# Layer 1 attention: context projections moved beside the layer norm, low parts taken by TensorE, four PSUM slots ahead of the first scores

## The reference

```python
x = x + jnp.tanh(g_xattn[1]) * _L1_xattn_ref(_layernorm(x), ctx_1024, ln_g, ln_b, Wq, Wkv, Wm, Wo, bo)

def _L1_xattn_ref(x, memories, ln_g, ln_b, Wq, Wkv, Wm, Wo, bo):
    xn = (x - mu) * rsqrt(var + EPS) * ln_g + ln_b      # a second norm, over the first
    q, kv, mem = xn @ Wq, xn @ Wkv, memories @ Wm       # mem: 6404 rows, from the context alone
    k = concatenate([k, mem]); v = concatenate([v, mem])
    attn = softmax(q @ k.T * 64 ** -0.5)                # 1024 x 7428 for each head
    return (attn @ v) reshaped @ Wo + bo
```

## Time and profile before

| | us |
|---|---|
| median of 3 runs | 5230.36 (5229.31 to 5230.93) |
| the profiled execution, its own time | 5229.35 |
| its span in the profile | 5227.6 |
| PE busy | 4813.3 (92%) |
| DVE busy | 4069.5 (78%) |
| ACT busy | 3357.1 (64%) |
| POOL busy | 1961.0 (38%) |

### The profile page before, as it was taken

The page is one execution under the profiler, slowest core; times in us unless marked ns, Lnnn a source line. Parts: engine busy times, 40 slices in busy tenths (PEclk is TensorE's granted clock), DMA queues, the critical chain, the costliest instruction groups (busy, mean ns, idle before and its releaser), DMA issues. The chain is left out here.

```text
span 5227.6 us, 76770 instructions
## 1 busy us (share of the span) xinstructions
PE 4813.3 (92%) x26366; PEld 1882.8 (36%) x26366; DVE 4069.5 (78%) x4870; ACT 3357.1 (64%) x6623; POOL 1961.0 (38%) x1522
## 2 busy tenths in 40 slices
PE   8938999999999999999994699999998699999997
PEld 5623454545445454544442222222222222222222
DVE  7646767677676767677776699999995599999996
ACT  3314565666666566656651388888885288888886
POOL 0015878787787878788782100000000100000000
PEclk9978999999999999999996799999998699999998
DMA  1024334242333334242210311111110211111110
GB/s 36 5 88 120 95 95 112 63 123 54 110 75 99 95 90 117 55 126 56 52 30 16 81 32 29 29 29 29 29 23 2 79 29 29 29 32 32 29 23 6
DMA packets 171390, 298.23 MB, mean 57 GB/s; under 512 B 39060, under 2 KB 108576, under 8 KB 167392
## 3 DMA queue, kind: packets, MB, share of 16 engines
q1 hardware_dynamic: 169420, 292.95, 22.0%
q10 hardware_dynamic: 1584, 0.37, 0.0%
HBM read 187.39 MB, written 101.25 MB: 55 GB/s over the span
## 5 line engine op out<-in xcount | busy, mean ns | idle before, releaser
L1856 ACT ACTIVATE a_prob<-ps 128x512 f32<-128x512 f32 (+1 forms) x3264 | 1699.4, 602 | 289.0 <-PE ps L1736 284.2
L1914 DVE TENSOR_REDUCE a_mx<-ps 128x1 f32<-128x1024 f32 x1536 | 1815.1, 1220 | 70.6 <-PE ps L1748 55.0
L1283 POOL TENSOR_TENSOR tot_p<-tot_p,prob 128x512 f32<-128x512 f32 (+1 forms) x922 | 1300.6, 1411 | 353.6 <-ACT prob L1141 267.6
L1748 PE MATMUL ps<-a_K,a_Q 59*128 59x512 bf16 (+1 forms) x3328 | 1094.7, 386 | 56.6 <-DMA a_Q<-q_stack_dram 44.7
L1141 ACT ACTIVATE prob<-ps 128x512 f32<-128x512 f32 (+1 forms) x1512 | 801.4, 609 | 511.7 <-PE ps L1007 510.7
L1736 PE MATMUL ps<-a_Q,a_K 59*128 59x512 bf16 (+1 forms) x3264 | 988.7, 383 | 55.3 <-ACT a_prob L1856 49.1
L1772 PE MATMUL ps<-a_prob,a_V 128*9 128x512 f32 x6528 | 872.1, 596 | 10.9 <-ACT a_acc L1840 10.9
L1006 PE MATMUL ps<-QA,KA 128*128 128x512 f32 (+1 forms) x1888 | 841.7, 446 | 0.0
L1018 PE MATMUL ps<-prob,V 128*64 128x512 f32 x3024 | 801.1, 599 | 0.7 <-ACT prob L1141 0.7
L1007 PE MATMUL ps<-QB,KB 128*128 128x512 f32 (+1 forms) x1888 | 746.6, 395 | 0.0
L1224 DVE TENSOR_TENSOR tot_d<-tot_d,prob 128x512 f32<-128x512 f32 x539 | 619.4, 1149 | 146.0 <-ACT prob L1141 129.5
(11 more groups left out here) (419 smaller groups left out, 4341.4 us busy)
## 6 DMA issues: line engine op xcount, KB each, us to landing
a_K<-k_stack_dram SPq DMA_DIRECT2D x128, 300.2 KB
k_hi_dram<-hi_s SPq DMA_DIRECT2D x112, 256.0 KB, 2.1
k_lo_dram<-lo_s SPq DMA_DIRECT2D x112, 256.0 KB, 2.4
KA<-k_hi_dram SPq DMA_DIRECT2D x64, 384.0 KB, 4.3
KA<-k_lo_dram SPq DMA_DIRECT2D x64, 384.0 KB, 5.6
KB<-k_hi_dram SPq DMA_DIRECT2D x64, 384.0 KB, 6.6
k_bf_dram<-bf_s SPq DMA_DIRECT2D x112, 128.0 KB, 1.8
KM<-k_bf_dram SPq DMA_DIRECT2D x32, 448.0 KB, 5.5
```

Of the source, the lines that this page charges most:

```text
L1283: nc.gpsimd.tensor_tensor(tot_p[0:r, u % 2, :], tot_p[0:r, u % 2, :], p, ALU.add).then_inc(totalled_p, 1)
L1748: last = nc.tensor.matmul(c.banks(slot(step) + half)[:, 0:k], Q[u % 3][MROW:MROW + ROWS, j * P:(j + 1) * P], K[(u // HALVES) % 2][MROW:MRO ...
L1856: nc.scalar.activation(prob[0:r, batch % 2, t % BATCH, :], c.banks(n % 3)[0:r, :], ACT.Exp, scale=SCALE).then_inc(exped, 1)
L1914: nc.vector.tensor_reduce(mx[:, u % 2, j, i % FULL:i % FULL + 1], c.banks(slot(step), 2), AX.X, ALU.max).then_inc(maxed, 1)
```

## The change

- The jobs of the context come first (k = 0 to 12), then q and k of x (13 to 16). `norm` is no longer a phase of its own for layer 1: DVE norms in the phase of the projections, while PE, ACT and POOL run the context's jobs.
- Since DVE is taken, the low part of the 13 context jobs of the first pair comes from PE: `take_hi` multiplies hi_s with the negative identity (`neg`, kept in QA[1]) and adds it to the job's PSUM; ACT copies what is left (`round_lo`). The 4 jobs of x still go by DVE.
- The two square roots stand in ACT's order behind jobs 3 and 7 (STD_BEHIND). Behind job 12 PE transposes h (`turn_h`), then waits for DVE's copy to hT.
- Up to the last maximum step of unit 0 there are four slots: banks 4 and 5, 6 and 7, 0 and 1, 2 and 3; after it again two.
- SP waits for KM and QM of head 0 to land before it issues `load_q` and the segments.
- gain and shift lie in fin_s.

```diff
+    MEM_JOBS = len(jobs)
+    jobs += [(W_Q, c.hT, a, n, [(a, 0, n)]) for a, n in chunks_of(N)]
+    jobs += [(W_K, c.hT, a, n, [(MEM + a, 0, n)]) for a, n in chunks_of(N)]
+    STD_BEHIND = (3, 7)
...
     def slot(n):
-        return 4 + 2 * (n % 2)
+        return (4, 6, 0, 2)[n % 4] if n < WIDE_SLOTS else 4 + 2 * (n % 2)
+
+    def before_slot(n):
+        return n - 4 if n < WIDE_SLOTS else n - 2
...
-            norm(c, gain, shift)
...
                 load_max(0)
+                sp.wait_ge(max_in_0, 96)
                 load_q(0)
...
+                def take_hi(k):
+                    m = jobs[k][3]
+                    pe.wait_ge(hi_out, k + 1)
+                    nc.tensor.matmul(c.banks(slot(slot_no["k", k]))[:, 0:m], neg, hi_s[k % DEPTH][:, 0:m],
+                                     start=False, stop=True, skip_group_check=True).then_inc(rest_ready, 1)
+
+                def turn_h():
+                    bank = take_slot(slot_no["turn", 0])
+                    pe.wait_ge(h_ready, 1)
+                    for t in range(QT):
+                        last = nc.tensor.transpose(c.banks(bank, 2)[:, t * P:(t + 1) * P], c.h[:, t, :], c.ident[:])
+                    last.then_inc(slotted, 1)
+                    pe.wait_ge(hT_ready, 1)
+
                 for k in range(JOBS):
+                    if k == MEM_JOBS:
+                        turn_h()
                     project(k)
-                    if k < GROUPS:
-                        project_v(0, k)
+                    if v_with(k) is not None:
+                        project_v(0, v_with(k))
+                    if k < MEM_JOBS:
+                        take_hi(k)
...
+                def round_lo(k):
+                    n, m = slot_no["k", k], jobs[k][3]
+                    act.wait_ge(rest_ready, k + 1)
+                    nc.scalar.copy(lo_s[k % DEPTH][:, 0:m], c.banks(slot(n))[:, 0:m]).then_inc(v_out, 1)
...
                 for k in range(JOBS):
                     round_hi(k)
-                    if k < GROUPS:
-                        take_v(0, k)
+                    if k < MEM_JOBS:
+                        round_lo(k)
+                    if v_with(k) is not None:
+                        take_v(0, v_with(k))
+                    if k in STD_BEHIND:
+                        root(STD_BEHIND.index(k))
...
-                for k in range(JOBS):
+                for k in range(MEM_JOBS, JOBS):
                     cut_lo(k)
```

More of the change, by code:

```diff
@@ L654, in l1_attention @@
     k_hi, k_lo, k_bf, q_hi, q_lo, q_bf = scratch
-    jobs = [(W_Q, c.hT, a, n, [(a, 0, n)]) for a, n in chunks_of(N)]
-    jobs += [(W_K, c.hT, a, n, [(MEM + a, 0, n)]) for a, n in chunks_of(N)]
+    jobs = []
     for a, n in chunks_of(S):
@@ L710, in takes_slot @@
         slot_no[kind, what] = len(slot_no)
-        by_act, count = kind in ("v", "fin"), [0, 0] if not freed else list(freed[-1])
+        by_act = kind in ("v", "fin") or (kind == "k" and what < MEM_JOBS)
+        count = [0, 0] if not freed else list(freed[-1])
         count[by_act] += 1
@@ L715, in l1_attention @@
     for k in range(JOBS):
+        if k == MEM_JOBS:
+            takes_slot("turn", 0)
         takes_slot("k", k)
-        if k < GROUPS:
-            takes_slot("v", (0, k))
+        if v_with(k) is not None:
+            takes_slot("v", (0, v_with(k)))
     for n in range(STEPS + LEAD):
         takes_slot("max", divmod(n, STEPS))
+    WIDE_SLOTS = slot_no["max", (0, STEPS - 1)] + 1
     for u in range(UNITS):
@@ L839, in l1_attention, with _ @@
-        fin_s, den = sb("fin_s", [P, CH]), sb("den1", [P, UQ])
+        fin_s, den = sb("fin_s", [P, CH]), sb("den1", [P, UQ])
+        gain, shift = fin_s[:, 0:D], fin_s[:, D:2 * D]
+        neg = QA[1][:, 0:P]
+        row_sum, var, rstd, tmp = (c.stat[:, i, :] for i in range(4))
+        with phase(nc, "loaded") as (block, loaded):
+            @block.sync
+            def _(sp):
+                sp.dma_start(gain, w["ln_g"].partition_broadcast(P)).then_inc(loaded, 16)
+                sp.dma_start(shift, w["ln_b"].partition_broadcast(P)).then_inc(loaded, 16)
+                sp.dma_start(bo[:], w["bo"].partition_broadcast(P)).then_inc(loaded, 16)
+                for base in (0, DH):
+                    sp.dma_start(Wo_twice[0][base:base + DH, :], w["Wo"][0:DH, :]).then_inc(loaded, 16)
+                sp.wait_ge(loaded, 16 * 9)
+            @block.scalar
+            def _(act):
+                act.dma_start(weights[0][:, W_Q, :], w["Wq"][:, 0:P]).then_inc(loaded, 16)
+                act.dma_start(weights[0][:, W_K, :], w["Wkv"][:, 0:P]).then_inc(loaded, 16)
+                act.dma_start(weights[0][:, W_V, :], w["Wkv"][:, HEADS * DH:HEADS * DH + P]).then_inc(loaded, 16)
+                act.dma_start(weights[0][:, W_M, :], w["Wm"][:, 0:P]).then_inc(loaded, 16)
+                nc.scalar.activation(neg, c.ident[:], ACT.Copy, scale=-1.0)
+            @block.vector
+            def _(dve):
+                nc.vector.memset(ones_col[:], 1.0)
+                nc.vector.memset(V[:, TILES - 1, :], 0.0)
+                for tile in QB:
+                    nc.vector.memset(f32(tile[DH:P, :]), 0.0)
+            @block.gpsimd
+            def _(pool):
+                nc.gpsimd.memset(f32(KB[DH:P, :]), 1.0)
@@ L873, in store @@
                         sp.dma_start(hi_to[p, :, to:to + m], f32(hi_s[k % DEPTH][:, frm:frm + m])).then_inc(done, 16)
-                    sp.wait_ge(released, freed[slot_no["k", k]][0])
+                    if k < MEM_JOBS:
+                        sp.wait_ge(v_out, freed[slot_no["k", k]][1])
+                    else:
+                        sp.wait_ge(released, freed[slot_no["k", k]][0])
                     for to, frm, m in parts:
@@ L946, in take_slot @@
                 def take_slot(n):
[L947 to L948 removed]
+                    if before_slot(n) >= 0:
+                        by_dve, by_act = freed[before_slot(n)]
                         if by_act:
@@ L1150, in take_extra, with root @@
                         take_fin(what)
+                def round_lo(k):
+                    n, m = slot_no["k", k], jobs[k][3]
+                    act.wait_ge(rest_ready, k + 1)
+                    nc.scalar.copy(lo_s[k % DEPTH][:, 0:m], c.banks(slot(n))[:, 0:m]).then_inc(v_out, 1)
+                def root(r):
+                    act.wait_ge(var_ready, r + 1)
+                    nc.scalar.activation(rstd, var, ACT.Sqrt).then_inc(std_ready, 1)
                 for k in range(JOBS):
                     round_hi(k)
-                    if k < GROUPS:
-                        take_v(0, k)
+                    if k < MEM_JOBS:
+                        round_lo(k)
+                    if v_with(k) is not None:
+                        take_v(0, v_with(k))
+                    if k in STD_BEHIND:
+                        root(STD_BEHIND.index(k))
                 for n in range(STEPS + LEAD):
```

42 lines of the change are left out of this document (39 added, 3 removed).

## The result

Four runs before gave a median of 5230.64 us (5229.31 to 5230.93), four of the changed kernel 5193.75 us (5192.08 to 5195.90). The forecast was 32.

A forecast was written before the change was run, and what follows sets the result against it. PE bounds the long loop of units, so an earlier first score moves the end equally. The terms brought that score from 438.41 to 405.7, 32.7 us, less 0.7 for DVE and POOL: 5198 us, range 5193 to 5206.

The forecast's parts named there:

- The ring through ACT: Context jobs: ACT's rounding, PE's product, ACT's low part and values follow each other and set a period of 2.4 us.
- Term 1: Start of the projections: PE starts at about 321.8 us, once POOL's memset releases the barrier behind `loaded`.
- Term 2: Thirteen context jobs: 2.4 us per job, second rounding at 327.4, rounding of job 12 at 353.8.
- Term 3: PE's transposes of h behind job 12: at full clock without waiting for h, jobs on x start at 357.1.
- The cover: Norm beside the context jobs: y is cleared by 350.5 and needed by 354.5, 4 us to spare.
- The rival that the clock falls at the turn: PE idles 1.6 us for DVE's copy; transposes and last jobs at half clock cost 1.0 + 5.9: 5205; chance 0.09.
- Term 4: Last four jobs and stores: about 5.9 us of jobs, last rounding at 363.0, KM issued at 367.0.
- Term 5: Loads of KM and QM: alone they need 7.3 us instead of 8.99; PE starts the maxima at 374.3.
- Term 6: First maxima: with four slots DVE is the bound, 27.0 us for 33.25, gain 6.2.
- The price on DVE: Norm beside POOL's casts: passes stretch by some 3 us, mostly in the cover; 0.7 us taken off the gain.
- The 3 us at the root: Second square root: if each DVE pass waited for a whole cast, ACT would wait up to 3 us: 5201.
- The list of rivals: Chances beside the forecast's 0.64: maxima unchanged 0.08, clock 0.09, norm bound 0.08, more gain 0.06, slower 0.03, no change 0.02.

The follow-up runs named there:

- e1: The kernel before with only the four slots, up to the last maximum step of unit 0: 5210.85 us against 5228.68.
- e2: The changed kernel with the two slots of before everywhere: 5212.27 us, ratio 0.9971 to the kernel before.
- e3: The changed kernel with the norm back in a phase of its own ahead of the projections: 5213.39 us, ratio 0.9973 to the kernel before.
- e11: The changed kernel with KM's context part loaded early in three pieces and POOL's memset of KB's lower half moved out of the first phase: 5192.44 us.
- e5: The changed kernel with the second square root behind job 10 instead of job 7: 5200.96 us, ratio 0.9944 to the kernel before.
- e7: The changed kernel with KM's context part loaded in two transfers ahead of job 14's stores: 5197.32 us, ratio 0.9937 to the kernel before.
- e4: The changed kernel without SP's wait for KM and QM before queries and segments are issued: 5196.45 us, ratio 0.994 to the kernel before.
- e6: The changed kernel with two slots in the projections and four from the first maximum step on: 5206.36 us, ratio 0.9957 to the kernel before.
- e9: The changed kernel run once more, unaltered, as a base for later runs: 5193.27 us against 5227.00 for the kernel before.

## Why the prediction was right, and where its sizes were off

- **The mechanism holds, but for the first term.** The ring through ACT set the jobs, the turn was covered, DVE bounded the maxima, and the loop of units gave nothing back. The two parts of the change are shown apart and add up: four slots alone 17.2 us (e1), all else alone 17.8 (e2), both 35.1. The path by e1 and e3 (17.2, then -3.4, then 21.3) gives 35.1 too, but it must, since each step starts where the last one ends.
- **Term 1, PE's start, was right by luck.** Forecast 7.0, measured 7.19. The prediction has the barrier released by POOL's memset; e11 shows that it is released by SP's wait for its transfers, which ends soon after.
- **Term 2, the thirteen jobs, was mis-sized.** I had 2.4 us per job; it is 2.15. The product takes 0.50 us and not the 0.41 of L1006, but ACT's low part, values and next rounding start 0.48 us apart and not 0.61. The eleven periods took 23.85 us with the two roots in them instead of 26.4, 2.6 less, and the second rounding was 0.6 earlier after PE's start than forecast. I had read ACT's durations where the distances of their starts were wanted; the earlier trace rows hold the lesson for PE, where the job's matmuls last 1.10 us and the values start 0.93 after them.
- **Term 3, the turn, was right, and in part by luck.** Transposes at full clock without a wait, 2.4 us from their start to PE's next job. h was ready at 350.4 us, 3.7 ahead. The cover was needed: in e5 a wait of 2.5 us came with 2.6 more through the clock. The rival that the clock falls at the turn, which had a chance of 0.09, came true in e7, whose kernel is the same up to there: of eight traces in which PE did not wait for h, seven kept the full clock behind the turn's 1.37 us and e7 did not. It cost 1.7 us there and not the 6.9 that the rival had, since the clock was back after two jobs.
- **Term 4, last jobs and stores.** The four jobs took 5.5 us (forecast 5.9), but from the last rounding to KM's issue there are 5.2 and not 4.0; the prediction's own parts (0.58, 0.72, two issues of 0.4, 2.3) add up to 4.4. The jobs follow each other in 1.75 us now, and the stores arrive at 86% of what the transfers can do, at 315 GB/s (second row of the stages above); in e5, where they come more slowly, the same step took 4.0.
- **Term 5, the load, failed.** I gave 7.3 us to the load alone; it takes 8.75, and 8.97 in company (e4). The 1.25 MB take 5.9 us at about 210 GB/s, where I had 5.6, and about 1.6 us pass before the first data, where I had 1.7; what I left out is the 1.2 us from the last data to PE's start. SP's wait does not pay.
- **Term 6, the maxima.** 25.6 us, forecast 27.0: DVE is the bound, and e1 and e6 give the same 25.6 with other work before it. The size was off for the reason of term 2. The same 46 instructions keep DVE busy for 24.83 us and not 26.17, with hardly another duration (0.69 us for the mean of L1197 in both, 1.22 for the reductions of two banks): one starts before the last has ended, now that none waits for PE.
- **The price on DVE was too high.** I had taken 0.7 us. POOL and DVE do meet: a pass of the norm that took 1.23 us alone takes 1.51 at two places where a cast falls on it, and the casts, 0.61 us in the median before, take up to 1.69:

```profile
347.66 1.23 DVE L1315 TENSOR_TENSOR h<-h,fin_s 128x1024 f32<-128x1024 f32 x1
...
347.68 1.69 POOL L1356 CAST bf_s<-hi_s 128x512 bf16<-128x512 f32 x1 [1.54 <-ACT hi_s L1125]
...
348.92 1.51 DVE L1316 TENSOR_TENSOR h<-h,fin_s 128x1024 f32<-128x1024 f32 x1
...
349.83 1.08 POOL L1356 CAST bf_s<-hi_s 128x512 bf16<-128x512 f32 x1 [0.47 <-ACT hi_s L1125]
```

The first cast starts with a DVE pass and ends 0.48 us after it, the next DVE pass ends 0.28 us late. This is the exclusive interface that the Trainium skill describes ("SBUF — State Buffer", section "Who interferes with whom": a DVE instruction with two SBUF inputs against a GpSimd one that reads SBUF); the trace agrees with it, with 1.69 for 0.61 us. But it is mostly POOL that waits, whose casts have room, and the root found its variance ready (344.64) when ACT came (344.76). The 3 us at the root that the rule could have cost did not come, though with only 0.12 us to spare.

The errors go both ways, and that half of them cancel is luck. Gains over the forecast: 3.1 us in the first jobs (term 2), 0.2 at the turn, 0.4 in the last four jobs, 1.4 in the maxima, 0.1 behind them, and the 0.7 of the price. Losses: 0.2 in PE's start, 1.2 in the stores, 1.4 in the load. The difference is the 3 us by which the shift of 35 is larger than 32. The first set of runs gained another 1.5 to 2, the second 1.4 less than the shift. (The list of rivals leaves 0.95 for faster and 0.02 for no change, where the prediction's last line has 0.94 and 0.03; nothing hangs on it.)

## What to carry to other kernels

Before moving work beside other work, look at the slots: here two more pairs of PSUM banks, in a stretch in which they lay idle, gave half of the gain by a few changed lines, and they gave it with the overlap or without. When an engine runs one instruction after another, take the distance of their starts for a period, not their length. A load moved ahead is only free where the queue is empty: the same 768 KB won 3.0 us and lost 3.5 in one place, won 2.9 and lost 1.8 in three others. And before a position in one profile is put down to an edit, compare the stages ahead of it: 3.3 of e7's 3.8 us and 1.4 of e5's 5.6 were there before the edit could act.

## What was not expected of the hardware

Executions of the same instructions differ by TensorE's clock in a place that the change does not touch. At 73 us, in layer 0, PE starts a row of products behind some 1.2 us of idle time. In the trace of before it runs at full clock there, in the one after at the lower level for six microseconds, and everything later is 2.6 us late:

```profile
73.30 0.50 PE L466 MATMUL ps<-Q_hi,K_hi 128*128 128x512 f32 x1 [1.20 <-ACT nmT L531]
...
73.64 0.39 PE L467 MATMUL ps<-Q_hi,K_lo 128*128 128x512 f32 x1
```

```profile
73.17 0.80 PE L466 MATMUL ps<-Q_hi,K_hi 128*128 128x512 f32 x1 [1.20 <-ACT nmT L531]
...
73.76 0.63 PE L467 MATMUL ps<-Q_hi,K_lo 128*128 128x512 f32 x1
```

The first fence is the timeline of before, the second that of after. The phase `loaded` starts between 313.3 and 317.5 us over the profiles of this study. The changed kernel's own two profiles have it at 317.4 and, in e9, at 315.1. This is likely much of why the runs of one kernel spread over 4 us, and it is why single stages were compared by their distance from a common start.

The second is the rate of the transfers: KM, read in pieces of 1 KB, moves at about 200 GB/s with the transfers full, while the stores of the last keys move at almost 400 in single microseconds and 360 over five. Two windows of the changed kernel's load, and two of e7's stores:

```profile
371.00:372.00 1.00, 0.00 (x0) 0.00 (x0) 0.00 (x0) 0.00 (x0) 0.00 (x0) 0.50 1.06 194
372.00:373.00 1.00, 0.00 (x0) 0.00 (x0) 0.00 (x0) 0.00 (x0) 0.00 (x0) 0.50 1.16 236
```

```profile
367.00:368.00 1.00, 0.00 (x0) 0.00 (x0) 0.00 (x0) 0.00 (x0) 0.00 (x0) 0.62 1.05 397
368.00:369.00 1.00, 0.00 (x0) 0.00 (x0) 0.00 (x0) 0.00 (x0) 0.00 (x0) 0.50 1.07 400
```

The runs don't tell whether it is the direction or the size of the pieces that halves the rate.
